# Layers 1 to 3 of a graph network kernel: the messages of a chunk by two multiplications instead of one, and gathers that wait for their own half

## The chip, the cores and the metric

The kernel runs on one core of a Trainium2 chip. The time is that of one execution on the device, in microseconds. The profiled execution gives the trace; a few more executions without a profile give the median.

## The reference

Four graph layers follow each other on 6250 nodes with 128 features. All use the same 206250 directed edges (100000 in both directions and one loop per node), sorted by their target node. After each layer x = layernorm(x + layer(x)).

```python
# layer 0: a network on each edge, mean over the edges of a target
msg_in   = concat(x[src], x[tgt], edge_features)
messages = relu(msg_in @ W1 + b1) @ W2 + b2
agg      = segment_sum(messages, tgt) / counts
...
# layers 1, 2, 3: attention with 4, 4 and 8 heads
h     = x @ W
e     = leaky_relu(a_s[src] + a_d[dst], 0.2)
m     = segment_max(e, dst)
p     = exp(e - m[dst])
alpha = p / segment_sum(p, dst)[dst]
out   = segment_sum(h[src] * alpha, dst)
```

In layer 1 the reference adds a second loop edge per node, which is kept apart from the 206250 edges, and so the kernel also sums up one more value per head there (eight columns more).

## The kernel before

The edges are cut into tiles of 128 and the tiles into 124 chunks of K = 13. Each of the four layers runs over its 124 chunks, two to a loop turn, since all large buffers have two places (b = 0 and 1). Between two layers stands a node stage that makes the new features and the table of rows (`rows1`, `rows2`, `rows3`) from which the next layer gathers.

What happens to one chunk c of layers 1 to 3, by engine:

- **GpSimd** (POOL, function `edges` at L557) issues 13 gathers for the chunk (L563). Each fetches 128 rows of the table, by the indices of one tile, into `G[:, b, t]`. Before the first of them it waits for the indices and for the counter `messages` of chunk c - 2 (L560), which used the same places in `G`.
- **ScalarE** (ACT) waits until all 13 gathers have landed and copies the source scores out of `G` (L921, the copy `shared<-G`).
- **TensorE** (PE, `attention` at L761) transposes these scores onto the target scores (L763), turns the membership matrices of chunk c + 1 (L699), spreads the maxima at the tile ends (L768, L777), makes the target scores of chunk c + 1 (L756, first 8 tiles, then the other 5), turns the weights (L787), spreads a factor (L791) and then sums the messages: `sums`, 13 products (L709) of the membership matrix with the messages, two tiles to a PSUM window.
- **VectorE** (DVE, `attention` at L1274) makes the membership matrix of chunk c + 1 in three parts (L1172; each waits for the sums of chunk c - 1 that still read its place), runs the scans and maxima, adds the window sums of chunk c - 1 (L1252), and last multiplies all gathered rows with the weights: one instruction over 13 tiles of 136 values (L1345), after which `messages` goes up.

Nothing is scheduled by a planner. The order on each engine is the order in which its block is written, and engines meet only at the counters. Each counter starts at 1, and `past(l, c)` is its value when chunk c of layer l is done. On TensorE the messages of a chunk are awaited after all that it does for the next chunk's target scores:

```python
                pe.wait_ge(fac_less, gpast(l, c))
                mm(ps_fac, memb[0:1, b, 0:P], factor[0:1, 2 * H:4 * H], start=True, stop=True).then_inc(fac_out, 1)
                pe.wait_ge(messages, past(l, c))
                if l == 1:
                    pe.wait_ge(maxf_kept, gpast(l, c))
                sums(l, c, b, SW if l == 1 else MW, None)
```

Layer 0 has a network in the place of the attention. It shares `edges` on GpSimd and `sums` on TensorE, and its VectorE part raises `messages` by an instruction of its own at the end of a chunk.

Of the kernel before, what the change touches and what calls it, by code (L numbers as in the profile page):

```python
# [5 lines left out]
def gnn_program(nc, A, out):  # L6
# [13 lines left out]
    ALU = mybir.AluOpType  # L20
# [26 lines left out]
    HALF = 8  # L47
    PARTED = [(0, 6), (6, 11), (11, K)]
# [8 lines left out]
    with ctx:  # L57
# [204 lines left out]
        messages = chunk_sem("messages_ready")  # L262
        summed = [chunk_sem(f"window_sums_of_part{p}_ready") for p in range(3)]
# [265 lines left out]
        def _(pool):  # L529
# [27 lines left out]
            def edges(l, c, b, h, early=False):  # L557
                pool.wait_ge(idx_loaded[b], 16 * (PAIRS * l + h + 1))
                if not early:
                    pool.wait_ge(messages, past(l, c - 2))  # L560
                pool.sem_inc(gather_paced, 1)
                for t in range(K):
                    nc.gpsimd.indirect_dma_start(  # L563
                        G[:, b, t, 0:rows[l].shape[1]], None, rows[l],
                        bass.IndirectOffsetOnAxis(idx[:, b, t:t + 1], 0)).then_inc(gathered[l][b], 16)
# [83 lines left out]
        def _(pe):  # L649
# [53 lines left out]
            def sums(l, c, b, width, parts):  # L703
                if c is not None:
                    pe.wait_ge(added[GR - 1], past(l, c - 1))
                for k in range(K):
                    if l == 0 and k in (0, 4, 8, 12):
                        pe.wait_ge(hidden[k // 4], past(0, c))
                    last = mm(ps_sum[k // 2][:, 0:width], memb[:, b, k * P:(k + 1) * P],  # L709
                              msg[:, b, k, 0:width], start=k % 2 == 0, stop=k % 2 == 1 or k == K - 1)  # L710
                    for p in range(3):
                        if k + 1 == PARTED[p][1]:
                            last.then_inc(summed[p], 1)
# [47 lines left out]
            def attention(l, c, b, ahead=True):  # L761
# [30 lines left out]
                pe.wait_ge(messages, past(l, c))  # L792
# [341 lines left out]
        def _(dve):  # L1134
# [119 lines left out]
            def mlp(c, b, h, prev=True, ahead=True):  # L1254
# [14 lines left out]
                dve.wait_ge(pre_added[3], past(0, c))  # L1269
                dve.sem_inc(messages, 1)  # L1270
# [4 lines left out]
            def attention(l, c, b, h, prev=True, ahead=True):  # L1275
# [66 lines left out]
                if prev:  # L1342
                    add_sums(l, c - 1, win, 5, GR)
                dve.wait_ge(wgt_turned, gpast(l, c))
                tt(msg[:, b, :, 0:MW].rearrange("p k (h f) -> p k h f", h=H),  # L1345
                   G[:, b, :, 0:MW].rearrange("p k (h f) -> p k h f", h=H),
                   ps_wgt.rearrange("p (h k) -> p k h", h=H).unsqueeze(3).to_broadcast([P, K, H, FW]),
                   ALU.mult).then_inc(messages, 1)
# [338 lines left out]
```

## Time and profile before

| | |
|---|---|
| median of 3 executions | 8771.89 us (8764.04 to 8781.84) |
| profiled execution | 8773.27 us |
| span from the first to the last instruction | 8771.2 us |
| TensorE clock granted, mean | 0.828 |
| busy: GpSimd, TensorE, VectorE, ScalarE | 6267.6, 6428.0, 5143.8, 2062.1 us |
| gathers issued | 6448 |

Busy times count the execution of instructions, not the waits between them, and GpSimd is counted as idle in the short stretch ahead of each gather. The profile names instructions by engine, line and operation; `out<-in` are the program's buffers. The four layers run, by the first and last gather of each, from 63 to 2118 us, from 2267 to 4338 us, from 4511 to 6533 us and from 6642 to 8664 us; between them stand the node stages.

### The profile page before, as it was taken

How to read it: one execution, taken by the hardware profiler on the slowest of the kernel's cores; microseconds unless marked ns; L12 is line 12 of the kernel's file. 1: busy time of each engine (PE TensorE's matmuls, PEld its weight loads, DVE VectorE, ACT ScalarE, POOL GpSimd, SP SyncE). 2: the span in 40 equal slices, each digit the busy share in tenths (PEclk: the TensorE clock that was granted, in tenths of full speed). 3: DMA queues.
4: the chain of work that ended last, by engine and by line, in shares of the span. 5: the costliest groups of instructions: out<-in, count | busy, mean ns of one | idle time of the engine just before them, and what ended most of it. 6: DMA issues, size and time to landing. Idle time of an engine off the chain costs nothing.

```text
span 8771.2 us, 141279 instructions
## 1 busy us (share of the span) xinstructions
PE 6428.0 (73%) x41611; PEld 5776.8 (66%) x41612; DVE 5143.8 (59%) x13620; ACT 2062.1 (24%) x7255; POOL 6267.6 (71%) x6594
## 2 busy tenths in 40 slices
PE   5777777777677777777777777777766777777775
PEld 4777777776566666666656666666655666666664
DVE  3333333334766666666676666666666666666666
ACT  2222222222322222222132222222222222222222
POOL 4777777776677777777657777777765777777774
PEclk7888888888888888888768888888877888888886
DMA  3333333332322222222232222222222222222222
GB/s 101 78 80 78 80 78 80 78 80 66 77 68 68 68 67 66 67 67 68 65 80 69 69 70 69 70 69 70 69 62 73 69 69 69 69 69 69 69 70 50
DMA packets 425473, 625.68 MB, mean 71 GB/s; under 512 B 189634, under 2 KB 305617, under 8 KB 425293
## 3 DMA queue, kind: packets, MB, share of 16 engines
q0 software_dynamic: 206336, 462.61, 22.5%
q1 hardware_dynamic: 219086, 162.49, 7.0%
q8 instruction: 20, 0.33, 0.0%
q14 instruction: 31, 0.25, 0.0%
HBM read 598.03 MB, written 26.58 MB: 71 GB/s over the span
## 4 chain that ended last, share of the span: by engine, by line
POOL 42%; issue 23%; PE 16%; DVE 11%; DMA 4%; DVEq 2%; SPq 1%; ACT 1%; POOLq 0%; ACTq 0%
POOL G L563 41%; PE ps L756 6%; PE ps L709 5%; DMA G<-rows,idx 3%; DVE msg L1345 2%; DVE acc L1252 2%; DVEq L1226 1%; DVE memb L1172 1%; PE ps L728 1%; PE ps L731 1%; PE ps L777 1%; DVE acc L1242 1%; DVE shared L1299 1%; DVE shared L1307 1%; DMA idx<-in_src 1%
## 5 line engine op out<-in xcount | busy, mean ns | idle before, releaser
L563 POOL DMA_INDIRECT G<-rows,idx x6448 | 6126.2, 950 | 2132.6 <-issue 1922.6
L756 PE MATMUL ps<-membT,shared 128*104 128x128 f32 x9672 | 1867.2, 370 | 2.2 <-ACT membT L921 2.2
L709 PE MATMUL ps<-msg,memb 128*128 128x136 f32 (+2 forms) x12896 | 1706.3, 291 | 101.3 <-DVE msg L1345 98.0
L756 PEld LDWEIGHTS ps<-membT,shared 128*104 128x104 f32 x9672 | 1705.6, 248 | 20.1 <-issue 3.0
L709 PEld LDWEIGHTS ps<-msg,memb 128*128 128x128 f32 x12896 | 1623.7, 199 | 128.0 <-issue 66.8
L1172 DVE TENSOR_TENSOR memb<-rel,ps 128x768 f32<-128x768 f32 x1488 | 1044.2, 730 | 1096.2 <-PE ps L709 1094.3
L1252 DVE TENSOR_TENSOR acc<-acc,ps 128x136 f32 (+2 forms) x3472 | 1024.5, 295 | 558.4 <-DVE acc L1252 347.1
L699 PE MATMUL ps<-ident,memb 128*128 128x128 f32 x6448 | 991.5, 292 | 153.8 <-DVE memb L1172 98.4
L728 PE MATMUL ps<-shared,membT 128*128 x3224 | 742.5, 317 | 493.3 <-DVE msg L1265 447.1
L921 ACT ACTIVATE membT<-ps 128x512 f32<-128x512 f32 x1984 | 948.0, 505 | 56.8 <-PE ps L699 52.8
L699 PEld LDWEIGHTS ps<-ident,memb 128*128 128x128 f32 x6448 | 768.9, 149 | 286.4 <-issue 183.0
L728 PEld LDWEIGHTS ps<-shared,membT 128*128 128x128 f32 x3224 | 577.5, 224 | 539.5 <-issue 539.5
L1345 DVE TENSOR_TENSOR msg<-G,ps 128x1768 f32<-128x1768 f32 x372 | 742.6, 1996 | 256.2 <-PE ps L787 253.5
L1265 DVE TENSOR_TENSOR msg<-G,ps 128x512 f32<-128x512 f32 x496 | 280.5, 586 | 767.2 <-PE ps L731 427.9
L731 PE MATMUL ps<-w1e,shared 128*128 128x128 f32 x3224 | 716.4, 309 | 0.0
L777 PE MATMUL ps<-ones,shared 1*104 1x1 f32 x1488 | 239.1, 261 | 601.2 <-DVE shared L1307 601.0
L921 ACT ACTIVATE shared<-G 128x104 f32<-128x104 f32 x372 | 140.5, 378 | 2260.2 <-DMA G<-rows,idx 2260.2
L777 PEld LDWEIGHTS ps<-ones,shared 1*104 1x104 f32 x1488 | 218.2, 217 | 682.7 <-DVE ps L1304 682.7
L958 ACT ACTIVATE msg<-msg 128x512 f32<-128x512 f32 x496 | 268.0, 549 | 1547.1 <-DVE msg L1265 1546.4
L731 PEld LDWEIGHTS ps<-w1e,shared 128*128 128x128 f32 x3224 | 581.6, 225 | 0.0
L768 PE MATMUL ps<-ident,shared 104*1 104x104 f32 x1488 | 204.5, 262 | 408.1 <-DVE shared L1289 407.8
L921 ACT ACTIVATE shared<-shared 128x8 f32 x2604 | 344.1, 216 | 495.9 <-issue 494.1
(182 smaller groups left out, 4552.6 us busy)
## 6 DMA issues: line engine op xcount, KB each, us to landing
G<-rows,idx POOLq DMA_INDIRECT x6448
shared<-marks_all SPq DMA_DIRECT2D x372, 156.0 KB
shared<-in_edge_attr SPq DMA_DIRECT2D x124, 256.0 KB
shared<-in_edge_attr SPq DMA_DIRECT2D x124, 160.0 KB
rows<-msg SPq DMA_DIRECT2D x36, 288.0 KB, 2.7
idx<-in_src SPq DMA_DIRECT2D x496, 6.5 KB
xrows<-msg SPq DMA_DIRECT2D x24, 256.0 KB, 2.2
memb<-xrows SPq DMA_DIRECT2D x24, 256.0 KB, 3.2
```

The costliest lines, as they stand in the source:

```text
L563: nc.gpsimd.indirect_dma_start(G[:, b, t, 0:rows[l].shape[1]], None, rows[l], bass.IndirectOffsetOnAxis(idx[:, b, t:t + 1], 0)).then_inc(g ...
L699: last = nc.tensor.transpose(ps_mT[j % 2][:, o:o + P], memb[:, b, k * P:(k + 1) * P], ident[:, :])
L709: last = mm(ps_sum[k // 2][:, 0:width], memb[:, b, k * P:(k + 1) * P], msg[:, b, k, 0:width], start=k % 2 == 0, stop=k % 2 == 1 or k == K - 1)
L728: mm(o, membT[:, k, :], btab[:, bass.ds(win[k // 2], 1), :].rearrange("p o f -> p (o f)"), start=True, stop=False)
L731: last = mm(o, ef[:, b, (k - h * HALF) * P:(k - h * HALF + 1) * P], w1e[:, h, :], start=False, stop=True)
L756: last = mm(ps_sc[b][0:JH, :], adz[:, k // 2, K - 1 - k:K - 1 - k + JH], membT[:, k, :], start=k == 0, stop=False)
L777: last = mm(ps_col[0:JH, w:w + 1], carry[0:1, w * JH:(w + 1) * JH], ones[0:1, 0:1], start=True, stop=True)
L921: return nc.scalar.activation(dst, src, ACT.Copy)
L1172: last = tt(memb[:, b, k0 * P:k1 * P].rearrange("p (k n) -> p k n", k=n), r, w, ALU.is_equal)
L1252: tt(a, a, ps_sum[g][:, 0:width], ALU.add).then_inc(added[g], 1)
L1265: o = tt(msg[:, b, k0:k1, 0:P], G[:, b, k0:k1, 0:P], ps_pre[j % 2][:, 0:(k1 - k0) * P].rearrange("p (k f) -> p k f", k=k1 - k0), ALU.add)
L1345: tt(msg[:, b, :, 0:MW].rearrange("p k (h f) -> p k h f", h=H), G[:, b, :, 0:MW].rearrange("p k (h f) -> p k h f", h=H), ps_wgt.rearrange( ...
```

## The change

The one multiplication of layers 1 to 3 becomes two, over tiles 0 to 5 and over tiles 6 to 12. The first raises a new counter, `first_messages`, the second raises `messages`. GpSimd waits for `first_messages` of chunk c - 2 ahead of gather 0, and for `messages` ahead of gather 6. TensorE waits for `first_messages` ahead of the sums, and for `messages` ahead of tile 6. In layer 0 VectorE raises both counters at the same place. The buffers, the sizes and the arithmetic stay.

```diff
+    FIRST = 6
...
             def edges(l, c, b, h, early=False):
                 pool.wait_ge(idx_loaded[b], 16 * (PAIRS * l + h + 1))
                 if not early:
-                    pool.wait_ge(messages, past(l, c - 2))
+                    pool.wait_ge(first_messages, past(l, c - 2))
                 pool.sem_inc(gather_paced, 1)
                 for t in range(K):
+                    if t == FIRST and not early:
+                        pool.wait_ge(messages, past(l, c - 2))
+                        pool.sem_inc(gather_paced, 1)
                     nc.gpsimd.indirect_dma_start(
...
                         pe.wait_ge(hidden[k // 4], past(0, c))
+                    if l and k == FIRST:
+                        pe.wait_ge(messages, past(l, c))
...
-                pe.wait_ge(messages, past(l, c))
+                pe.wait_ge(first_messages, past(l, c))
...
                 dve.wait_ge(pre_added[3], past(0, c))
+                dve.sem_inc(first_messages, 1)
                 dve.sem_inc(messages, 1)
...
                 dve.wait_ge(wgt_turned, gpast(l, c))
-                tt(msg[:, b, :, 0:MW].rearrange("p k (h f) -> p k h f", h=H),
-                   G[:, b, :, 0:MW].rearrange("p k (h f) -> p k h f", h=H),
-                   ps_wgt.rearrange("p (h k) -> p k h", h=H).unsqueeze(3).to_broadcast([P, K, H, FW]),
-                   ALU.mult).then_inc(messages, 1)
+                for k0, k1, done_with in ((0, FIRST, first_messages), (FIRST, K, messages)):
+                    tt(msg[:, b, k0:k1, 0:MW].rearrange("p k (h f) -> p k h f", h=H),
+                       G[:, b, k0:k1, 0:MW].rearrange("p k (h f) -> p k h f", h=H),
+                       ps_wgt.rearrange("p (h k) -> p k h", h=H)[:, k0:k1, :].unsqueeze(3)
+                       .to_broadcast([P, k1 - k0, H, FW]), ALU.mult).then_inc(done_with, 1)
```

GpSimd's loop over the chunks of layer 1, before (a row is an instruction with its line, what it writes and reads, its size, and the counters for which it waits; x12 means twelve alike):

```order
L634 ISA
L560 ISA [waits indices_loaded0]
L563 DMA G<-rows,idx 128x144 [waits messages_ready]
L563 DMA G<-rows,idx 128x144 x12
L560 REGISTER_ALU [waits indices_loaded1]
```

and the same place with the change:

```order
L639 ISA
L562 ISA [waits indices_loaded0]
L568 DMA G<-rows,idx 128x144 [waits messages_of_first_tiles_ready]
L568 DMA G<-rows,idx 128x144 x5
L568 DMA G<-rows,idx 128x144 [waits messages_ready]
L568 DMA G<-rows,idx 128x144 x6
L562 REGISTER_ALU [waits indices_loaded1]
```

The wait for the whole chunk's messages has moved from the first gather to the seventh; the first waits for the new counter.

TensorE at the end of a chunk of layer 1, before:

```order
L787 MATMUL ps<-ident,shared 128x104 [waits weights_ready]
L756 MATMUL ps<-membT,shared 104x128 [waits membership_turned_kept3,membership_turned_kept2]
L756 MATMUL ps<-membT,shared 104x128 x4
L791 MATMUL ps<-shared,memb 128x16 [waits factor_less_one_ready]
L709 MATMUL ps<-msg,memb 128x144 [waits window_sums_added6,first_maxima_kept,messages_ready]
L709 MATMUL ps<-msg,memb 128x144 x12
```

and with the change:

```order
L794 MATMUL ps<-ident,shared 128x104 [waits weights_ready]
L763 MATMUL ps<-membT,shared 104x128 [waits membership_turned_kept3,membership_turned_kept2]
L763 MATMUL ps<-membT,shared 104x128 x4
L798 MATMUL ps<-shared,memb 128x16 [waits factor_less_one_ready]
L716 MATMUL ps<-msg,memb 128x144 [waits window_sums_added6,first_maxima_kept,messages_of_first_tiles_ready]
L716 MATMUL ps<-msg,memb 128x144 x5
L716 MATMUL ps<-msg,memb 128x144 [waits messages_ready]
L716 MATMUL ps<-msg,memb 128x144 x6
```

The order of the products is the same; only what the first of them waits for has changed, and the seventh has a wait that it had not.

## Rows read from the trace of the kernel before

**Rows 1.** The page: busiest line, and the chain that ended last.
```profile
POOL 42%; issue 23%; PE 16%; DVE 11%; DMA 4%; DVEq 2%; SPq 1%; ACT 1%; POOLq 0%; ACTq 0%
...
L563 POOL DMA_INDIRECT G<-rows,idx x6448 | 6126.2, 950 | 2132.6 <-issue 1922.6
```
**Rows 2.** Timeline of POOL: first gather of chunks 0 and 123, layers 1, 2.
```profile
2267.06 1.02 POOL L563 DMA_INDIRECT G<-rows,idx  x1 [10.06 <-DMA rows<-msg]
...
4322.56 0.94 POOL L563 DMA_INDIRECT G<-rows,idx  x1 [0.30 <-issue]
...
4511.05 1.05 POOL L563 DMA_INDIRECT G<-rows,idx  x1 [8.63 <-DMA rows<-msg]
...
6517.50 0.95 POOL L563 DMA_INDIRECT G<-rows,idx  x1 [0.30 <-issue]
```
**Rows 3.** Waits of POOL in layer 1: total us, times, longest us.
```profile
POOL G L563 <- DVE msg L1345: 58.8, 62, 2.8
```
**Rows 4.** Timeline, chunks 31 and 32 of layer 2 on POOL: start, duration, idle before.
```profile
5028.53 2.00 DVE L1345 TENSOR_TENSOR msg<-G,ps 128x1768 f32<-128x1768 f32 x1 [0.50 <-PE ps L787]
...
5031.85 0.94 POOL L563 DMA_INDIRECT G<-rows,idx  x1 [0.30 <-issue]
5033.10 0.96 POOL L563 DMA_INDIRECT G<-rows,idx  x1 [0.30 <-issue]
5034.36 0.94 POOL L563 DMA_INDIRECT G<-rows,idx  x1 [0.30 <-issue]
```
**Rows 5.** Timeline of all engines, end of chunk 64 of layer 1.
```profile
3364.62 2.43 PE L756 MATMUL ps<-membT,shared 128*104 128x128 f32 x10
3364.84 2.00 DVE L1345 TENSOR_TENSOR msg<-G,ps 128x1768 f32<-128x1768 f32 x1 [1.86 <-PE ps L787]
...
3367.52 4.15 PE L709 MATMUL ps<-msg,memb 128*128 128x144 f32 x26
3367.62 0.94 POOL L563 DMA_INDIRECT G<-rows,idx  x1 [2.72 <-DVE msg L1345]
...
3371.51 0.38 PE L763 MATMUL ps<-ident,shared 128*104 128x128 f32 x2
```
**Rows 6.** The same view, end of chunk 65 of layer 1.
```profile
3380.80 2.00 DVE L1345 TENSOR_TENSOR msg<-G,ps 128x1768 f32<-128x1768 f32 x1
...
3381.95 0.39 PE L791 MATMUL ps<-shared,memb 1*128 1x16 f32 x2
...
3382.93 4.96 PE L709 MATMUL ps<-msg,memb 128*128 128x144 f32 x26 [0.59 <-DVE msg L1345]
```
**Rows 7.** Windows at the ends of chunks 64 and 65: length, busy PE PEld DVE ACT POOL, clock, DMA.
```profile
3364.00:3368.00 4.00, 3.63 (x15) 3.29 (x16) 2.00 (x1) 0.86 (x4) 1.28 (x2) 0.50 0.26 75
3380.00:3384.00 4.00, 2.96 (x17) 2.64 (x18) 2.63 (x5) 0.49 (x3) 2.98 (x4) 0.83 0.38 96
```
**Rows 8.** Waits of PE: two rows of layer 1, then one of layer 2 (total, times, longest).
```profile
PE ps L709 <- DVE msg L1345: 30.3, 54, 0.7
PE ps L763 <- ACT shared L921: 15.8, 9, 11.5
...
PE ps L763 <- ACT shared L921: 114.2, 117, 10.0
```
**Rows 9.** Groups of VectorE in layer 1, shapes apart.
```profile
L1345 DVE TENSOR_TENSOR msg<-G,ps 128x1768 f32<-128x1768 f32 x123 | 245.6, 1996 | 88.7 <-PE ps L787 88.3
L1172 DVE TENSOR_TENSOR memb<-rel,ps 128x768 f32<-128x768 f32 x123 | 117.4, 955 | 345.7 <-PE ps L709 345.7
```
**Rows 10.** Timeline of POOL: two first gathers, chunks 74 and 82, layer 1.
```profile
3504.15 0.94 POOL L563 DMA_INDIRECT G<-rows,idx  x1 [2.73 <-DVE msg L1345]
...
3640.71 0.94 POOL L563 DMA_INDIRECT G<-rows,idx  x1 [2.72 <-DVE msg L1345]
```
**Rows 11.** Timeline, end of the last chunk of layer 1.
```profile
4353.28 5.17 PE L709 MATMUL ps<-msg,memb 128*128 128x144 f32 x20 [1.55 <-DVE msg L1345]
```
**Rows 12.** Timeline of DVE: the two shorter membership parts back to back (640, 256 elements).
```profile
3387.55 1.15 DVE L1172 TENSOR_TENSOR memb<-rel,ps 128x640 f32<-128x640 f32 x2 [0.27 <-PE ps L709]
```

More of the change, by code:

```diff
@@ L262, in gnn_program @@
         messages = chunk_sem("messages_ready")
+        first_messages = chunk_sem("messages_of_first_tiles_ready")
         summed = [chunk_sem(f"window_sums_of_part{p}_ready") for p in range(3)]
```

## The prediction, made before the changed kernel ran

> **What bounds the kernel now.** I read the page first, then the gathers layer by layer, then the waits of GpSimd, and last the timelines of single chunks. The chain that ended last runs over GpSimd for 42% of the span, and its gathers keep it busy for 6126.2 us in 6448 issues [rows 1]. A gather starts 1.25 us after the one before it, so a chunk of 13 costs GpSimd 16.3 us. The boundary between two chunks, with its waits and its counter step, costs no more than any other gather: from the last gather of chunk 31 at 5031.85 to the first of chunk 32 at 5033.10, and then to 5034.36, two pitches of 1.25 us [rows 4]. From the first gather of chunk 0 to that of chunk 123, layer 2 takes 6517.50 - 4511.05 = 2006.5 us and layer 1 takes 4322.56 - 2267.06 = 2055.5 us [rows 2]. Layer 1 is therefore the only one of the three whose gathers are held up, by 49 us, and the view of waits names what holds them: `DVE msg L1345`, 58.8 us in 62 cases, of which 0.30 us each is the ordinary pause [rows 3]. That leaves some 40 us of true waiting (summed boundary by boundary I get 42). In layer 2 the messages of chunk 30 end at 5030.53 and are wanted by the gather at 5033.10, 2.57 us later [rows 4]; going through all chunks, this distance is at least 1.03 us in layer 2 and 1.95 in layer 3. A gather that does wait starts 0.78 us after the multiplication's end: 3364.84 + 2.00 to 3367.62 [rows 5].
>
> Why are layer 1's messages late? In layer 2 TensorE waits for landed gathers (the scalar copy) ahead of its score product 117 times, 114.2 us. In layer 1 it does so 9 times [rows 8]: there the product starts as soon as the sums of the chunk before end. So layer 1 is bound by the round sums, scores, scans, weights, messages, sums. GpSimd only feels it where a few slow rounds add up. The slow rounds are those at half clock: the ten target products take 2.43 us in one chunk (granted clock 0.50, the 1.2 GHz level) and in the next the stretch is at 0.83 with the end of the round at full speed [rows 5 to 7].
>
> **The multiplication.** 1768 elements take 1996 ns and 768 take 955 ns [rows 9], so an element costs 1.041 ns and an instruction 0.155 us besides. The halves of 816 and 952 elements then take 1.005 and 1.146 us. Two such instructions back to back overlap a little: 640 and 256 elements, 0.82 + 0.42 by the same formula, took 1.15 us together, 0.09 less [rows 12]. So the first tiles are ready 1.0 us sooner than all were, the rest 0.06 us later than before. Who reads the rest? TensorE's tile 6 and gather 6. The sums begin 1.5 us after the multiplication's start at the earliest (below) and the rest is ready at 2.1; six tiles at 4.15 / 13 = 0.32 us [rows 5] take longer than the 0.6 us between, even at twice the speed. Gather 6 comes 7.5 us after gather 0. So the 0.06 us cost nothing. Bounds: 0, and 124 x 0.06 = 7.4 us if all of it stood on layer 1's round; I take 0. The Trainium skill ("VectorE: DVE Perf Modes", the section on the TRN2 errata) says that each instruction pays its fixed part anew, some 150 cycles, and that small tiles should be avoided. As an estimate from its figure, 0.156 us for each of layer 1's 124 chunks would be 19 us if it were on the path; this trace agrees on the size of the fixed part (0.155 us) but shows a wait for TensorE right behind the multiplication, which covers it.
>
> **The added waits.** GpSimd gets one wait and one counter step more in each of 488 chunks. The boundary rows show what the same pair costs when it is satisfied: nothing beyond the pitch [rows 4]. Bounds 0 and, at the 0.01 us to which the rows are printed, 5 us; I take 0. If it did show, it would show in all four layers alike. TensorE gets a satisfied wait between tile 5 and 6. Bounds: 0, and 0.05 us x 124 = 6 us in layer 1, where TensorE is the bound; layer 0's sums have three such waits and show no gap, so 0. The extra counter step on VectorE in layer 0 lies ahead of a long idle; 0.
>
> **Gathers released earlier.** A late gather now starts 1.0 + 0.78 us after the multiplication's start, not 2.0 + 0.78. This alone doesn't make the round of layer 1 any shorter. GpSimd gets 1.0 us at the first wait of a slow stretch and then meets the same late messages. In layers 2 and 3 nothing waited: 0.
>
> **Sums begun earlier.** This is the larger part. At full clock TensorE is through with its other work at 3381.95 + 0.39 and stands idle for 0.59 us for the messages [rows 6]; the first half would be there at 3381.8. It saves 0.6 us. At half clock the last other product ends after the multiplication, and the sums begin without any wait (3367.52) [rows 5]: it saves nothing. The waits of TensorE count how often each is so: 54 of 124 chunks in layer 1, 30.3 us, longest 0.7 [rows 8]. So 54 x 0.6 = 32 us is the most that this can give; VectorE's membership parts, which wait for the sums, follow along.
>
> **The sum.** I went through layer 1 chunk by chunk with the trace's own durations and three rules: a first gather comes 13 of its own pitches after the last one or 0.78 us after the first half, whichever is later; a score product comes when its copy is done or the sums before it end; the sums end 0.6 us sooner in the 54 chunks. The early release alone gives 3.5 us, the earlier sums alone 7.9, both 19.1. They need each other, because what the round gains is used only if the gathers may follow, and is lost where GpSimd is not waiting. In one cycle of eight chunks, from 3367.62 to 3504.15, the walk gives 1.7 us: its three chunks at full clock times 0.6. At the end of a layer the sums of the last chunk waited 1.55 us [rows 11]; 1.0 of it goes, in each of three layers, 3 us. Layers 0, 2 and 3 are otherwise unchanged. Together 22 us of 8773.3: 8751.2 for an execution like the profiled one, which lay 1.4 us over the median. I forecast 8750. A difference under 0.2%, 17.5 us, can't be told from no change here; the forecast lies just beyond.
>
> **The rivals.**
> *TensorE's clock gives it back, or the gain stays at the release.* TensorE's half-clock chunks may fall elsewhere. If the added full-clock savings vanish, only the 3.5 us and the layer ends remain: 6.5 us, 8765. For it: 70 chunks of layer 1 save nothing, and the savings hang on which these are. Against: 54 waits are there to be taken.
> *GpSimd never waits in layer 1.* Then all 42 us of waiting go, and 3 at the ends: 8728. It needs rounds at full clock where there are half-clock ones now: the ten products alone are 2.43 us in one and 1.31 in the other. For it: the idle stretches of TensorE get shorter. Against: most of its idle time comes from VectorE's scans and stays. The Trainium skill ("TensorE: Matmul & The Clock Gate", on HAM oscillation) says that waits between groups of products throw the array back to half rate, so fewer waits would keep it up; this case's rows show the two levels side by side, not what decides between them.
> *Slower: the round locks into its slow pattern.* From 3367.62 to 3504.15 to 3640.71 the first gathers of every eighth chunk lie 136.5 us apart [rows 5, 10], 17.07 us per chunk. Layer 1 runs so only in part; its mean is 2055.5 / 123 = 16.71. If the earlier sums shift the phases so that all of it runs so, it takes 123 x 17.07 = 2100 us, 44 more, less the 22 of the change: 8795. It turns into a loss once over half of the remaining layer falls in. For it: the pattern repeats to 0.03 us, so it holds itself up once entered. Against: the change gives each such cycle 1.7 us, and other stretches of the layer are free of it.
> *It does nothing* is the first rival's extreme: 8772.
>
> **How the numbers follow.** The forecast's case, a gain of 12 to 30 us, gets 0.50; the gain near the release alone, 0 to 12 us, 0.27; no waiting at all 0.11; the slow pattern in some part 0.12. Faster by over 0.2% is two thirds of the forecast's case and all of the third: 0.44. Slower by over 0.2% is a bit over half of the last: 0.07. The rest, 0.49, is within. The range goes from 8728, where no gather waits, to 8782: half a slow pattern, or nothing gained and the 10 us by which one of the three executions lay above the median. The forecast's own case spans 8742 to 8760.
>
> **What would show it.** In the changed kernel the multiplication is two groups of 1.0 and 1.15 us. First gathers of layer 1 that wait start 1.8 us after the first one's start; gather 6 never waits. TensorE's waits for messages shrink from 54 cases of 0.56 us to next to none, and its sums begin 1.5 us after the multiplication's start at full clock. Layer 1 takes about 2036 us from first gather to first gather, layers 0, 2 and 3 the same as now within 2 us. I am wrong if layers 2 or 3 change by more, if the gathers' pitch isn't 1.25 us at gather 6, or if the number of half-clock chunks in layer 1 moves by more than ten.

## The result, and the profile after

| | before | changed |
|---|---|---|
| median | 8776.86 us (8764.04 to 8791.08, 6 runs) | 8719.90 us (8717.71 to 8727.65, 6 runs) |
| profiled execution, its span | 8773.27, 8771.2 us | 8727.65, 8725.9 us |
| TensorE clock granted, mean | 0.828 | 0.822 |

The ratio is 0.9936 with an interval of 0.9924 to 0.9949: 0.6% faster, and beyond the range of the prediction on its low side. Both kernels were timed again together here, which is why the median of before isn't the one of the table further up.

The page of the changed kernel: the chain that ended last, then three of the busiest groups. The rows that answer to it are [rows 1].

```profile
POOL 46%; issue 25%; PE 12%; DVE 9%; DMA 4%; DVEq 2%; SPq 1%; ACT 1%; POOLq 0%; ACTq 0%
...
L568 POOL DMA_INDIRECT G<-rows,idx x6448 | 6121.7, 949 | 2093.7 <-issue 1931.0
...
L716 PE MATMUL ps<-msg,memb 128*128 128x136 f32 (+2 forms) x12896 | 1702.8, 291 | 1.7 <-DVE msg L1354 1.7
...
L1354 DVE TENSOR_TENSOR msg<-G,ps 128x816 f32<-128x816 f32 x744 | 766.5, 1071 | 237.5 <-PE ps L794 235.4
```

The gathers cost what they did, to 4 us in 6126, and the chain lies on GpSimd more than before. TensorE's sums wait for messages 1.7 us in the whole program. The multiplication is now 744 instructions, which take 1071 ns in the mean. With the shapes apart, those of layer 1 take 1004 and 1139 ns, for which 1.005 and 1.146 us were forecast.

The timeline of GpSimd, first gathers of chunks 0 and 123 of layer 1 and of layer 2 (start, duration, idle before), against [rows 2]:

```profile
2263.19 1.02 POOL L568 DMA_INDIRECT G<-rows,idx  x1 [8.39 <-DMA rows<-msg]
...
4279.30 0.94 POOL L568 DMA_INDIRECT G<-rows,idx  x1 [0.30 <-issue]
...
4468.73 1.04 POOL L568 DMA_INDIRECT G<-rows,idx  x1 [8.62 <-DMA rows<-msg]
...
6476.57 0.94 POOL L568 DMA_INDIRECT G<-rows,idx  x1 [0.30 <-issue]
```

Layer 1 takes 2016.1 us from first gather to first gather where it took 2055.5: 39.4 us less. Layer 2 takes 2007.8 for 2006.5, layer 3 2006.0 for 2006.4, layer 0 2039.6 for 2040.5. So 39.4 of the 45.6 us between the two profiled executions lie in layer 1. The rest is spread over the start, layer 0 and the stretches between and behind the layers, each 0.9 to 2.3 us shorter but one, which is 0.9 longer, as layer 2 is by 1.4.

The waits in layer 1 (total us, times, longest us), against [rows 3, 8]:

```profile
PE ps L770 <- ACT shared L928: 25.0, 23, 8.2
POOL G L568 <- DVE msg L1354: 14.5, 24, 2.6
```

GpSimd waits for messages 24 times where it did 62 times. Summed over the boundaries and less the ordinary pitch, that is 8.6 us for 42.7. TensorE's own waits for messages ahead of the sums (54 of them before) have no row left. In their place TensorE waits for landed gathers more often, 23 times for 9.

A round at full clock, in chunk 5 of layer 1, TensorE and VectorE, against [rows 6]:

```profile
2375.42 1.31 PE L763 MATMUL ps<-membT,shared 128*104 128x128 f32 x10
2375.51 2.06 DVE L1354 TENSOR_TENSOR msg<-G,ps 128x816 f32<-128x816 f32 x2
2376.66 0.39 PE L798 MATMUL ps<-shared,memb 1*128 1x16 f32 x2
2376.98 3.45 PE L716 MATMUL ps<-msg,memb 128*128 128x144 f32 x26
2378.87 0.95 DVE L1179 TENSOR_TENSOR memb<-rel,ps 128x768 f32<-128x768 f32 x1 [1.30 <-PE ps L716]
```

The two multiplications take 2.06 us together, the sums begin 1.47 us after their start with no idle time ahead, and take 3.45 us. In [rows 6] they began 2.13 us after it, behind 0.59 us of idle time, and took 4.96 us.

Those 4.96 us are not the length of sums at full clock. The windows over the idle time, the first 3.13 us of these sums, their rest, and the whole, in the trace of before (stretch, length, busy PE PEld DVE ACT POOL, clock, DMA), and then the window over the changed kernel's sums:

```profile
3382.34:3382.93 0.59, 0.00 (x2) 0.01 (x1) 0.46 (x1) 0.00 (x0) 0.33 (x1) 0.75 0.19 71
3382.93:3386.06 3.13, 3.13 (x13) 3.13 (x14) 0.00 (x0) 0.38 (x1) 2.49 (x3) 0.50 0.32 71
3386.06:3387.89 1.83, 1.83 (x17) 1.83 (x16) 1.29 (x2) 0.90 (x7) 1.25 (x2) 1.00 0.23 44
3382.93:3387.89 4.96, 4.96 (x28) 4.96 (x28) 1.29 (x2) 1.28 (x8) 3.74 (x5) 0.69 0.28 61
...
2376.98:2380.43 3.45, 3.45 (x29) 3.45 (x28) 1.88 (x3) 0.38 (x1) 2.54 (x4) 1.00 0.29 71
```

The granted clock fell from the 2.4 GHz level to the 1.2 GHz level within the idle time, stayed there for the first 3.1 us of the sums and rose again within them. The sums of 3.45 us are granted 1.00 throughout.

A late gather, the first of chunk 45, which waits for the multiplication of chunk 43, a round whose target products are at half clock, against [rows 5]:

```profile
3001.32 2.43 PE L763 MATMUL ps<-membT,shared 128*104 128x128 f32 x10
3001.53 2.06 DVE L1354 TENSOR_TENSOR msg<-G,ps 128x816 f32<-128x816 f32 x2 [1.83 <-PE ps L794]
3003.32 0.94 POOL L568 DMA_INDIRECT G<-rows,idx  x1 [2.55 <-DVE msg L1354]
```

It starts 1.79 us after the multiplication's start, where it was 2.78.

To see where the time of layer 1 goes I cut its 123 rounds, from one multiplication's start to the next, into four pieces, and read each of them from the timelines of TensorE and VectorE. A round is called full where the stretch from the weights' transpose to the factor product (L787 to L791 before, L794 to L798 after) takes under 1.8 us, which is the 1.31 us of the ten target products at the 2.4 GHz level against 2.43 us at the 1.2 GHz level. All sums are us over 123 rounds, and the last column counts the last chunk's round too; kernels e1 to e15 are those of the experiments. Sums of 5.0 us stand for all from 4.9 to 5.1.

| kernel | start to sums | sums | sums' end to score product | score product to next start | together | full rounds, and of them with sums of 5.0 us |
|---|---|---|---|---|---|---|
| before | 298.4 | 489.6 | -14.0 | 1282.2 | 2056.2 | 55, 9 |
| changed | 277.3 | 489.8 | 1.6 | 1252.4 | 2021.1 | 44, 0 |
| e1 | 312.5 | 524.2 | -18.2 | 1274.9 | 2093.4 | 36, 29 |
| e2 | 313.3 | 535.8 | -20.2 | 1271.5 | 2100.4 | 34, 32 |
| e3 | 258.9 | 469.1 | 13.9 | 1270.8 | 2012.6 | 59, 0 |
| e4 | 299.9 | 489.4 | -11.6 | 1281.9 | 2059.5 | 52, 9 |
| e9 | 326.3 | 514.7 | -9.7 | 1317.0 | 2148.3 | 80, 0 |
| e10 | 302.7 | 520.5 | -17.0 | 1260.5 | 2066.7 | 32, 20 |
| e11 | 266.1 | 480.3 | 6.9 | 1258.4 | 2011.7 | 53, 0 |
| e12 | 328.0 | 577.6 | -16.6 | 1210.8 | 2099.8 | 2, 0 |
| e15 | 265.1 | 480.6 | 6.9 | 1262.4 | 2014.9 | 54, 0 |

The third piece is the wait for landed gathers; where the score product follows the sums at once, it overlaps their end by about 0.2 us, hence the minus. From before to the change the first piece gives 21.1 us, the second nothing, the third takes 15.6 back, and the fourth gives 29.8. That is 35.1 us from multiplication to multiplication; between the first gathers, which run up to two chunks ahead of it, it is the 39.4 us above.

The fourth piece is where the prediction has nothing. In layer 1 alone TensorE transposes a part of the maxima (L785), ScalarE copies the result, and only then makes the weights (it waits for this transpose 110 times, 244.5 us). The transpose is queued on TensorE behind the target products of the next chunk's first eight tiles. TensorE in two rounds of **before**, chunks 65 and 66 of layer 1:

```profile
3377.39 1.99 PE L756 MATMUL ps<-membT,shared 128*104 128x128 f32 x16
3379.32 0.31 PE L785 MATMUL ps<-ident,shared 104*128 104x104 f32 x1
...
3394.52 3.74 PE L756 MATMUL ps<-membT,shared 128*104 128x128 f32 x16
3398.06 0.38 PE L785 MATMUL ps<-ident,shared 104*128 104x104 f32 x1
```

Those sixteen take 1.99 us in one round, at a granted clock of 1.00, and 3.74 in the next, at 0.50, and the transpose (L785) follows 1.93 and 3.54 us after their start. So 1.6 us that come of the clock lie on the round there. Their mean over layer 1 is 2.84 us before and 2.65 after: 0.185 x 123 = 23 of the 29.8 us.

How the gain divides over the pieces differs from kernel to kernel, though. The four kernels whose sums begin on the first part of 3 or 6 tiles (changed, e3, e11, e15) take 2010.0 to 2016.1 us in layer 1, first gather to first gather, which is within 10 us of what the gathers alone take in layers 2 and 3. But in e3 the sums give 20 us and the fourth piece only 11 (its sixteen products still take 2.79 us), and the full rounds are 59 there, 53 in e11 and 54 in e15, whose layer 1 has the same instructions as that of the changed kernel with its 44. What the four have in common is the earlier start, no idle time ahead of the sums in a full round, and no sums of 5.0 us in one.

### The profile page after: what moved, and what is told of

It reads as the page before. It is cut to its first block, busy times and chain, and to the rows that moved or that the text cites. A ratio compares the mean times of both kernels' runs of the same rounds, so it can differ in the third digit from the quotient of the medians.

```text
span 8725.9 us, 142264 instructions
## 1 busy us (share of the span) xinstructions
PE 6436.7 (74%) x41611; PEld 5789.7 (66%) x41612; DVE 5169.7 (59%) x13992; ACT 2057.0 (24%) x7255; POOL 6262.9 (72%) x6594
## 4 chain that ended last, share of the span: by engine, by line
POOL 46%; issue 25%; PE 12%; DVE 9%; DMA 4%; DVEq 2%; SPq 1%; ACT 1%; POOLq 0%; ACTq 0%
POOL G L568 45%; PE ps L763 4%; PE ps L716 3%; DMA G<-rows,idx 3%; DVE acc L1259 1%; DVEq L1233 1%; PE ps L735 1%; PE ps L738 1%; DVE memb L1179 1%; DVE acc L1249 1%; PE ps L794 1%; DVE shared L1307 1%; DVE msg L1272 1%; DMA idx<-in_src 1%; DVE msg L1354 1%
## 5 line engine op out<-in xcount | busy, mean ns | idle before, releaser
L704 PE MATMUL ps<-ident,memb 128*128 128x128 f32 x6448 | 1018.4, 298 | 141.6 <-DVE memb L1179 89.2
L704 PEld LDWEIGHTS ps<-ident,memb 128*128 128x128 f32 x6448 | 793.3, 152 | 271.8 <-issue 172.7
L1354 DVE TENSOR_TENSOR msg<-G,ps 128x816 f32<-128x816 f32 x744 | 766.5, 1071 | 237.5 <-PE ps L794 235.4
```

The costliest lines, as they stand in the source:

```text
L704: last = nc.tensor.transpose(ps_mT[j % 2][:, o:o + P], memb[:, b, k * P:(k + 1) * P], ident[:, :])
L1354: tt(msg[:, b, k0:k1, 0:MW].rearrange("p k (h f) -> p k h f", h=H), G[:, b, k0:k1, 0:MW].rearrange("p k (h f) -> p k h f", h=H), ps_wgt.re ...
```

## The experiments

Edits are shown against the changed kernel unless another is named; none of them leaves out or alters part of the computation. Ratios are to before, timed in the same series. That is 8768.70 us (15 runs) for e1 to e4, 8771.09 (15 runs) for e9 to e12 and 8763.92 (9 runs) for e15 and e16.

**e1_split_only: two multiplications, but everybody waits for the second.**

```diff
-                    pool.wait_ge(first_messages, past(l, c - 2))
+                    pool.wait_ge(messages, past(l, c - 2))
...
-                pe.wait_ge(first_messages, past(l, c))
+                pe.wait_ge(messages, past(l, c))
```

> The two multiplications stay, but GpSimd and TensorE both wait for the second before they begin, as they did for the one. Every theory: what the second instruction costs, 0.06 us a chunk at the end of the messages, at most 7 us in layer 1: 8777 to 8784 against a before of 8777. If the theory that half-clock stretches of TensorE sit by chance in layer 1's rounds is right, such a small shift alone could move the time by 10 to 20 us either way; if it moves by under 8 us, chance placing is not strong.

8811.83 us (8807.60 to 8816.94), ratio 1.0049 (1.0035 to 1.0063): 43 us slower than before. The waits in layer 1:

```profile
POOL G L568 <- DVE msg L1354: 104.7, 83, 2.4
...
PE ps L716 <- DVE msg L1354: 21.9, 34, 0.7
```

and TensorE's factor products and sums in its timeline there:

```profile
3010.83 0.60 PE L798 MATMUL ps<-shared,memb 1*128 1x16 f32 x2
3011.37 3.97 PE L716 MATMUL ps<-msg,memb 128*128 128x144 f32 x26
...
3028.19 4.09 PE L716 MATMUL ps<-msg,memb 128*128 128x144 f32 x26
...
3044.99 4.22 PE L716 MATMUL ps<-msg,memb 128*128 128x144 f32 x26
...
3059.48 0.39 PE L798 MATMUL ps<-shared,memb 1*128 1x16 f32 x2
3060.52 4.97 PE L716 MATMUL ps<-msg,memb 128*128 128x144 f32 x26 [0.65 <-DVE msg L1354]
```

Three rounds at half clock follow each other with little variation, then one at full clock (0.39 us for the factor product against 0.60) in which TensorE idles 0.65 us and then needs 4.97 us for sums that take 3.45 in the changed kernel. This repeats through the layer at some 17.0 us a chunk: 29 of the 36 full rounds have such sums, 9 of 55 before. So the price was not the 7.4 us of my bound, nor the 10 to 20 us of chance placing, but 43 us, as layer 1 moved into another pattern of the clock. The messages are late by 0.06 us here. The two added waits are in this kernel too; neither shows a pause of its own (the seventh gather of a chunk starts 1.27 us after the sixth in layer 1, 1.28 before, and no sums have idle time inside), but no run separates them from the 0.06 us.

**e2_release_only: only GpSimd waits for the first half.**

```diff
-                pe.wait_ge(first_messages, past(l, c))
+                pe.wait_ge(messages, past(l, c))
```

> GpSimd's first six gathers wait for the first half only, TensorE's sums wait for all messages. Walk theory (rounds of layer 1 unchanged): 3.5 us faster, about 8773, and TensorE's idle time for messages stays 30 us in layer 1. Release theory (late gathers make late landings, which make late messages): the larger share of the 45 to 57 us, 8735 to 8745, with few POOL waits left. Clock theory (closing TensorE's gap ahead of the sums is what moves its half-clock stretches): no more than 10 us, since the gap stays.

8810.33 us (8807.39 to 8815.28), ratio 1.0047 (1.0034 to 1.0061). It is 1.5 us under e1: releasing the gathers 1.0 us sooner gives nothing that can be told from none, though 83 of them wait for messages in e1 and 60 here. No theory expected a loss against before, but it is 42 us slower, and TensorE's idle time ahead of the sums is still there (32 of 34 full rounds have the long sums).

**e3_sums_only: only TensorE waits for the first half.**

```diff
-                    pool.wait_ge(first_messages, past(l, c - 2))
+                    pool.wait_ge(messages, past(l, c - 2))
```

> TensorE begins the sums with the first half, GpSimd waits for all messages as before. Walk theory: 7.9 us in layer 1 and 3 us at the layers' ends, 11 faster, 8766. Clock theory: the eight target products of layer 1 (the stretch from the carry products to the turn of the maxima) shrink from 3.17 to about 2.95 us a chunk as in the changed kernel, and 30 to 45 us go, 8732 to 8747. Release theory: about 10 us.

8722.45 us (8720.43 to 8726.03), ratio 0.9948 (0.9934 to 0.9962), whose interval overlaps that of the whole change. The waits in layer 1:

```profile
PE ps L770 <- ACT shared L928: 36.4, 41, 9.9
POOL G L568 <- DVE msg L1354: 15.6, 38, 2.4
```

and the sums in the stretch shown for e1:

```profile
3026.54 0.39 PE L798 MATMUL ps<-shared,memb 1*128 1x16 f32 x2
3026.86 3.45 PE L716 MATMUL ps<-msg,memb 128*128 128x144 f32 x26
...
3042.91 3.45 PE L716 MATMUL ps<-msg,memb 128*128 128x144 f32 x26
...
3059.86 4.05 PE L716 MATMUL ps<-msg,memb 128*128 128x144 f32 x26
```

From e1 to e3, which differ in TensorE's wait alone, lie 89 us. By the table 54 come from the earlier start of the sums, 55 from shorter sums, 4 from the fourth piece, and 32 go back to waits for landed gathers (layer 1: 2093.4 - 2012.6 = 81). GpSimd's waits fall to those of the changed kernel though it waits for the whole multiplication: they go because the round gets shorter. The time is below the range of every theory, and the products that the clock theory named did not shrink as it said: the stretch from the carry products to the turn of the maxima takes 3.12 us for 3.16 before and 2.95 in the changed kernel.

**e4_before_again: the kernel before, as one more kernel of the series.**

> The kernel before, unchanged, with a second trace. All theories: the same median within 8 us. Its runs so far spread from 8764 to 8791, those of the changed kernel from 8718 to 8728; if the spread comes from where layer 1's slow pattern of eight chunks sets in, this trace's layer 1 shows another number of such cycles than the first one's, and layers 2 and 3 are the same within 2 us.

8771.04 us, ratio 1.0003 (0.9993 to 1.0012), and a cut of layer 1 like that of before (52 full rounds, 9 with long sums; 2053.8 us from first gather to first gather for 2055.5, layers 2 and 3 within 1 us). The two traces have as many long sums, so they don't show where the spread of before comes from. What the other kernels show in the table is their own.

**Two series that say little.** The next four kernels (e5 to e8, repeated below as e9 to e12), and later e13 and e14 (repeated as e15 and e16), ran in series in which before itself took 13004 us and 12364 us, the first on the chip of the same number as the next series with its 8771 us. The chain that ended last lies there for 29 to 34% on what the profile calls another core or an unknown queue, which has no share in any other trace of this case. VectorE stood still for it up to 15.6 us at a time, as in e7:

```profile
DVE shared L1307 <- remote: 2743.7, 361, 15.6
```

The edits are those shown below under e9 to e12, e15 and e16, and what was expected of them was:

> The kernel of e1 (two multiplications, all waits for the second), with the product that spreads the factor done three times into the same place instead of once, right ahead of the sums. At full clock this fills TensorE's 0.65 us gap with work; the sums begin no sooner. At half clock it delays them by about 1 us. Gap theory (the idle stretch ahead of the sums is what makes the clock fall within them): sums of 5.0 us after a full-clock stretch, 29 of 35 in e1, are nearly gone and take 3.45 us; in time -45 us for these and up to +80 for the delays at half clock, so 8780 to 8850, the durations decide. Start theory (only the earlier start matters, the clock falls with TensorE's share of work in the round): the 5.0 us sums stay as frequent as in e1, time 8830 to 8870.

> The changed kernel with the first part of 11 tiles instead of 6: it is ready 1.71 us after the start, so at full clock the sums begin about 1.8 us after it, not 1.47, with a gap of 0.3 us left, half of that before. Gap theory with a threshold between 0 and 0.3 us: the 5.0 us sums come back, time 8760 to 8800. Gap theory with the threshold above 0.3, or start theory with a gain that follows the start in proportion: no 5.0 us sums, layer 1 in between, 8730 to 8750.

> The changed kernel with the first part of 3 tiles: ready 0.58 us after the start. TensorE cannot begin sooner than it does now (it is busy until 1.47), so all theories in which TensorE's start decides say the same time as with 6, 8717 to 8728. GpSimd gets its first three gathers free 0.4 us sooner; if the release were worth its full time in the waits left in layer 1 (13 in the changed kernel), 2 to 5 us less.

> The changed kernel, with the target products of tiles 0 to 3 of the next chunk moved ahead of TensorE's wait for the carries, where it idles 1.9 us in layer 1; tiles 4 to 7 stay behind the carry products. Layer 1's round gets up to 1.2 us shorter from the carries to the maxima (2.95 us a chunk in the changed kernel, then about 1.9). If layer 1 is bound by this round, its last waits of GpSimd go and it takes 2006 us like layers 2 and 3: 5 to 10 us faster than the changed kernel, 8708 to 8715. If the carries come later at half clock or the clock falls more often, no gain.

> The changed kernel with two multiplications and the two waits in layer 1 alone; layers 2 and 3 as before. If layer 1 carries all: the same time as the changed kernel within 5 us, 8717 to 8730 against a before near 8770. If layers 2 and 3 carry part of the gain: between the two, 8735 to 8755.

> The changed kernel with the target products of tiles 8 to 12 moved from ahead of the sums to behind them, ahead of the next score product. The sums then begin 1.1 us after the multiplication's start at either clock (1.47 or 2.68 now), VectorE's membership parts come sooner, and TensorE's work in a round is the same. If VectorE's parts were on layer 1's round, it becomes as fast as layers 2 and 3: 2006 us and up to 10 us less than the changed kernel, 8710 to 8718. If TensorE's work alone bounds the round: no change, 8717 to 8730. If a wait of TensorE for the second half (ready 2.1 us after the start, six tiles at full clock are through by 2.7) or another placing of half-clock stretches comes in: up to 40 us slower, and the 5.0 us sums or half-clock sums would show it.

The ratios were 1.0191 (e5), 1.0030 (e6), 1.0143 (e7), 1.0300 (e8), 1.0154 (e13) and 1.0529 (e14), each within 0.3% either way. Layer 1 isn't bound there by what binds it here, so they decide nothing between the theories, and I draw nothing from them but this: e7 and e13, which gain 0.4 to 0.5% below, lost 1.4 to 1.5% there. Why is open, and so is what the change itself does under such conditions, since it wasn't run in these series.

**e9_split_filled: e1, with the factor product done three times.** The same product is written three times, so that TensorE has less idle time ahead of the sums.

```diff
-                mm(ps_fac, memb[0:1, b, 0:P], factor[0:1, 2 * H:4 * H], start=True, stop=True).then_inc(fac_out, 1)
+                for again in range(3):
+                    last = mm(ps_fac, memb[0:1, b, 0:P], factor[0:1, 2 * H:4 * H], start=True, stop=True)
+                last.then_inc(fac_out, 1)
```

> The kernel of e5 once more: its call fell on a chip on which the kernel before itself took 13004 us, with long waits between engines in all four layers, so that nothing there compares with the earlier traces. Gap theory: sums of 5.0 us after a full-clock stretch, 29 of 35 in e1, nearly gone, 3.45 us in their place; time 8780 to 8850. Start theory: the 5.0 us sums as frequent as in e1, 8830 to 8870.

8877.84 us (8860.57 to 8887.27, 4 runs), ratio 1.0125 (1.0109 to 1.0140). TensorE's timeline in layer 1:

```profile
3013.93 1.46 PE L799 MATMUL ps<-shared,memb 1*128 1x16 f32 x6
3015.32 5.56 PE L716 MATMUL ps<-msg,memb 128*128 128x144 f32 x26
...
3032.30 0.84 PE L799 MATMUL ps<-shared,memb 1*128 1x16 f32 x6
3033.34 3.45 PE L716 MATMUL ps<-msg,memb 128*128 128x144 f32 x26 [0.20 <-DVE msg L1356]
```

With 0.13 to 0.21 us of idle time in the place of 0.65 no full round has sums of 5.0 us (79 of the 80 take 3.45), and there are twice as many full rounds as in e1, although the sums begin no sooner. So the idle time is part of what makes the sums long. The filling doesn't pay, however: the time lies above the ranges of both theories. At half clock the three products take 1.46 us for 0.60 with no gap to fill, and the sums behind them take 5.3 to 5.6 us.

**e10_first_11 and e11_first_3: the cut after tile 10, and after tile 2.**

```diff
-    FIRST = 6
+    FIRST = 11
```

```diff
-    FIRST = 6
+    FIRST = 3
```

> The kernel of e6 once more, for the same reason. The first part has 11 tiles and is ready 1.71 us after the start; at full clock the sums begin about 1.8 us after it, a gap of 0.3 us. Gap theory with a threshold under 0.3 us: the 5.0 us sums come back, 8760 to 8800. Threshold above 0.3, or a gain that follows the start: none of them, 8730 to 8750.

> The kernel of e7 once more, for the same reason. First part of 3 tiles, TensorE's start can't move: 8717 to 8728 if TensorE's start decides; up to 5 us less if the earlier release of the gathers were worth its time.

e10: 8791.52 us (8772.79 to 8793.51), ratio 1.0021 (1.0012 to 1.0031); its profiled execution is the fastest of its eleven, so the trace shows it 19 us better than its median. e11: 8726.20 us (8717.33 to 8730.17), ratio 0.9950 (0.9937 to 0.9964). TensorE's timeline of e10:

```profile
3047.44 0.39 PE L798 MATMUL ps<-shared,memb 1*128 1x16 f32 x2
3048.13 5.12 PE L716 MATMUL ps<-msg,memb 128*128 128x144 f32 x26 [0.30 <-DVE msg L1354]
...
3099.88 3.45 PE L716 MATMUL ps<-msg,memb 128*128 128x144 f32 x26 [0.23 <-DVE msg L1354]
```

With eleven tiles in the first part 0.2 to 0.3 us of idle time stay, about half of what it was, and still 20 of 32 full rounds have the long sums: 0.2% slower than before, although its messages for the sums are ready sooner than before's. The rounds divide by their idle time: all 20 with 0.30 or 0.31 us have the long sums, all 11 with 0.23 us the short ones (the last round is cut off). With three tiles the idle time is gone as with six, and nothing more is to be had from the still earlier release.

**e12_moved_products: half of the first eight tiles' target products made where TensorE idles for the carries.**

```diff
+                if ahead:
+                    pe.wait_ge(sc_copied, gpast(l, c))
+                    target_scores(l, c + 1, 1 - b, 0, 4)
                 pe.wait_ge(run_kept, gpast(l, c))
...
-                    pe.wait_ge(sc_copied, gpast(l, c))
-                    target_scores(l, c + 1, 1 - b, 0, 8)
+                    target_scores(l, c + 1, 1 - b, 4, 8)
```

> The kernel of e8 once more, for the same reason. Four of the target products ahead of the wait for the carries: if layer 1 is still bound by its round, it takes 2006 us like layers 2 and 3, and the time is 8708 to 8715; if the carries come later at half clock or the clock falls more often, no gain or a loss.

8989.72 us (8987.66 to 8991.16), ratio 1.0249 (1.0235 to 1.0263). The timeline of TensorE in layer 1:

```profile
3006.41 1.04 PE L763 MATMUL ps<-membT,shared 128*104 128x128 f32 x8
3008.36 0.49 PE L787 MATMUL ps<-ones,shared 1*104 1x1 f32 x4 [0.91 <-DVE shared L1317]
3008.78 1.12 PE L763 MATMUL ps<-membT,shared 128*104 128x128 f32 x8
...
3012.11 2.43 PE L763 MATMUL ps<-membT,shared 128*104 128x128 f32 x10
3015.01 4.73 PE L716 MATMUL ps<-msg,memb 128*128 128x144 f32 x26
```

The move does what it was to do: the products at the transposes' side are down to 1.12 us and the fourth piece loses 42 us against the change. But 122 of 124 rounds of layer 1 are now at half clock, with sums of 4.4 to 4.9 us and no idle time ahead of them, and not only there: layers 2 and 3, which no other kernel so far moved, go from 2006 to 2091.6 us each, with some 120 rounds at half clock and sums of 4.7 to 5.2 us for 3.28. The same products in another place cost 270 us against the change, where a gain of 5 to 10 was expected.

**e15_layer1_only: the change in layer 1 alone.** Layers 2 and 3 have one multiplication and wait for `messages`, as before.

```diff
-                    pool.wait_ge(first_messages, past(l, c - 2))
+                    pool.wait_ge(first_messages if l == 1 else messages, past(l, c - 2))
...
-                    if t == FIRST and not early:
+                    if t == FIRST and l == 1 and not early:
...
-                    if l and k == FIRST:
+                    if l == 1 and k == FIRST:
...
-                pe.wait_ge(first_messages, past(l, c))
+                pe.wait_ge(first_messages if l == 1 else messages, past(l, c))
...
-                for k0, k1, done_with in ((0, FIRST, first_messages), (FIRST, K, messages)):
+                parts = ((0, FIRST, first_messages), (FIRST, K, messages)) if l == 1 else ((0, K, messages),)
+                if l > 1:
+                    dve.sem_inc(first_messages, 1)
+                for k0, k1, done_with in parts:
```

> The kernel of e13 once more, for the chip's sake. Layer 1 carries all: 8717 to 8730. Layers 2 and 3 carry part: 8735 to 8755.

8725.40 us (8721.78 to 8727.62), ratio 0.9956 (0.9942 to 0.9969). The interval overlaps that of the whole change. Layer 1 carries the gain as far as this can tell.

**e16_tail_after: the last five tiles' target products behind the sums.**

```diff
-                if ahead:
-                    target_scores(l, c + 1, 1 - b, 8, K)
                 pe.wait_ge(fac_less, gpast(l, c))
...
                 sums(l, c, b, SW if l == 1 else MW, None)
+                if ahead:
+                    target_scores(l, c + 1, 1 - b, 8, K)
```

> The kernel of e14 once more, for the chip's sake. VectorE's membership parts on the round: 8710 to 8718. TensorE's work alone bounds it: 8717 to 8730. Another placing of the half-clock stretches or a wait for the second half: up to 40 us slower, and the sums' durations would show it.

8993.46 us (8984.91 to 8995.64), ratio 1.0260 (1.0246 to 1.0274), mean clock 0.77. TensorE's waits in layer 1, and then two of its sums in the timeline:

```profile
PE ps L716 <- DVE msg L1354: 72.9, 112, 0.9
```

```profile
3014.63 4.93 PE L716 MATMUL ps<-msg,memb 128*128 128x144 f32 x26 [0.56 <-DVE msg L1354]
...
3030.75 5.12 PE L716 MATMUL ps<-msg,memb 128*128 128x144 f32 x26 [0.85 <-DVE msg L1354]
```

The idle time ahead of the sums is back in 112 rounds, and with it sums of mostly 4.9 to 5.1 us, at a factor product of 0.60 us or 0.39 alike. Layer 1 takes 2199.8 us, and layers 2 and 3 give way too, to 2046 and 2045. That is some 270 us more than the change, where at most 40 were expected. No kernel beats the change; e3, e11 and e15 are as good within their intervals.

## Why the prediction was right, and where it failed

- **What binds.** Right. Layer 1 is bound by the round of TensorE and VectorE, and layers 2 and 3 by GpSimd: the change moved layer 1 by 39.4 us and the others by at most 1.4, and e15, with the change in layer 1 alone, has the gain.
- **The multiplication.** The durations came out (1071 ns in the mean, 2.06 us for both), and gather 6 never waits. The price was taken as 0 with a bound of 7.4 us; e1, which has the two added waits as well, shows 43. The bound held the pattern of the clock fixed. In the changed kernel the price isn't to be seen, since nothing waits for the second half.
- **The added waits.** Right: gather 6 keeps the pitch of 1.25 us in layers 2 and 3, and TensorE has no row for its wait at tile 6.
- **The release alone, 3.5 us.** Right in size (e1 to e2: 1.5 us). That the release and the earlier sums need each other was wrong: e3 has the whole gain without the release, 46 us where the walk gave 7.9 and 3 at the ends.
- **Sums begun earlier.** Right in kind and per round: 0.66 us (2.13 to 1.47) for the forecast 0.6, and 21.1 us together of at most 32. The reading of [rows 6] under it was not right: the end of that round is not at full speed, since 3.1 us of its sums are granted 0.50. The prediction counted the 0.59 us of waiting and left the 1.5 us by which such sums are too long where they were.
- **The sum, and here the prediction failed.** The step is the walk through layer 1 "with the trace's own durations", which gave 19.1 us for what measured 39.4. It kept each round's clock, and with it the length of each burst of products, where it lay. The traces show that the clock, and with it these lengths, changes with the start of the sums. Sums of 5.0 us in full rounds, 9 before, are gone in every kernel whose sums begin on the first 3 or 6 tiles, and half-clock stretches fall elsewhere: in the changed kernel the first sixteen target products, with the transpose queued behind them, got 23 us shorter, in e3 it was the sums, by 20. Either way layer 1 comes down to within 10 us of what its gathers alone take, and there the gain ends. The walk gave this nothing, and no way of pricing it from the trace of before was found.
- **The sign of being wrong.** The full rounds went from 55 to 44, eleven, just over the ten that the prediction named as a sign against itself. They stay within four of 55 in e3, e11 and e15, which have the same gain, so this number tells of one execution rather than of the change. The mean clock, 0.828 to 0.822, is no measure of layer 1 either: by windows it goes from 0.84 to 0.83 there, and from 0.83 to 0.82 in layers 2 and 3, whose time did not move.
- **The ends of the layers.** 3 us forecast; the stretches outside layer 1 gave 6 us together in the two profiled executions, of which those around layer 0, where nothing was to change, are part. No run separates it.
- **The rivals.** The profiled execution, at 8727.65, landed on the 8728 of "GpSimd never waits in layer 1". It isn't quite that (8.6 us of waiting are left), and it got a chance of 0.11. It was to need rounds at full clock where there were half-clock ones, and in this trace it came about with fewer full rounds, in e3 with a few more. The slow pattern, given 8795, is real. It is what the halves do to the kernel when TensorE must wait for both (e1, e2: 8810 to 8812), and the earlier start of the sums is what keeps the changed kernel out of it. That the clock gives the gain back did not happen here; in e12 and e16 it did so many times over.

What stays open is what decides that the clock falls. In layer 1 every full round with long sums had idle time ahead of them, and without any idle time none had. But idle time alone does not do it. Layer 2 of before has it ahead of the sums in 63 rounds:

```profile
PE ps L709 <- DVE msg L1345: 31.4, 63, 0.8
```

The factor product ahead of these sums takes 0.39 us in all 63, as at full clock, and 60 of the sums take 3.28 us; only 3 take 4.8, and none of the 64 with idle time in layer 3. Nor does its size order the kernels: with 0.5 to 0.7 us before has 9 long in 54, with 0.57 to 0.65 e1 has 29 in 35, with 0.30 e10 has 20 in 20. So the time of none of these kernels could have been told beforehand. And since e9 closes the idle time and is slower for its added work, no run shows what closing it is worth by itself, apart from starting sooner.

## What to carry to other kernels

Where TensorE's round bounds a stage and its granted clock alternates, an estimate that keeps the trace's durations and shifts starts is off by as much as the effect itself: here a gain of 19 us came out as 39, and a cost of at most 7 as 43. Read the granted clock over each burst of products before taking its length as that at full clock. Look for short idle times right ahead of such a burst and take these away first, by letting the burst start on the part that is ready; the earlier release of buffers, on an engine that only feels the round, gave nothing measurable here. Before moving TensorE's products to another place in the round, run it: both moves tried here (e12, e16) cost more than 2%.

## What the runs showed of the hardware

- Sums of the same 13 tiles take 3.45 us at a granted clock of 1.00 throughout, or 4.9 to 5.1 us where the clock fell to 0.50 at most 0.4 us before or 0.3 us after they began, though the products ahead of them ran at full clock. So it was in all 99 long sums of full rounds in layer 1 of before, e4, e1, e2 and e10, with 0.30 to 0.66 us of idle time ahead. In the first 3.1 us of those in [rows 6] the clock is 0.50.
- A shift of 0.06 us a round in the end of VectorE's multiplication, with two satisfied waits beside it, changed the layer by 36 us (e4 to e1, first gather to first gather: 2053.8 to 2089.5 us).
- Layers 2 and 3, which GpSimd bounds with 1 to 2 us to spare, gave way as well once TensorE was at half clock in nearly all of their rounds (e12: 2006 to 2092 us).
